# A selective-scan block on one core: two tokens to a partition, and one transfer of 1 KB rows where there were two of 512 B

## The reference

```python
xn = _layernorm(x)
# branch 1: a state-space block with E = 256 channels, N = 64 states, followed by a gated FFN
normed = rmsnorm(xn, input_norm_w)
x_z, z = split(normed @ in_proj_W)                 # (8, 512, 256) each
xc = silu(conv(x_z, conv_W) + conv_b)              # 4 taps
dt = clip(softplus(xc @ dt_W + dt_b), 0.001, 0.1)
Bp, Cp = xc @ B_W, xc @ C_W                        # 64 states each
h_t = exp(dt_t * A) * h_{t-1} + dt_t * B_t * x_t   # 512 steps, state 256 x 64 per sequence
y_t = sum_n h_t * C_t
y = y * silu(z)
x1 = xn + y @ out_proj_W
n2 = rmsnorm(x1, ffn_norm_w)
branch1 = x1 + (silu(n2 @ gate_W) * (n2 @ up_W)) @ down_W
# branch 2: three layers with +-1 weights, 256 -> 512 -> 512 -> 128, relu between
branch2 = binary_mlp(xn)
out = x + branch1 + branch2
```

## Time and profile before

| | |
|---|---|
| median of 3 runs | 1047.95 us (1047.13 to 1048.22) |
| the profiled execution's own time | 1046.38 us |
| its span, first to last instruction | 1044.6 us |
| granted TensorE clock, mean over the span | 0.981 |
| busy, of the span | PE 90%, DVE 87%, ACT 86%, POOL 79% |
| busy share of the DMA engines through the recurrence | 0.95 to 0.98 |

### The profile page before, as it was taken

How to read it: one execution, slowest core, us unless ns; L and a number is a source line. 1 busy time by engine, 2 the same in 40 slices (tenths; PEclk the granted TensorE clock), 3 DMA queues, 4 the chain that set the end, 5 groups by cost and what they waited for, 6 DMA issues and landing times.

```text
span 1044.6 us, 24920 instructions
## 1 busy us (share of the span) xinstructions
PE 941.4 (90%) x8006; PEld 423.2 (41%) x8006; DVE 911.8 (87%) x1966; ACT 902.2 (86%) x1061; POOL 824.3 (79%) x1159
## 2 busy tenths in 40 slices
PE   5999984669999999999999999999999999999997
PEld 3566541123434343434333333434343434343436
DVE  5788965899999999999999999999999999999982
ACT  1766876799999999999999999999999999999981
POOL 5365325899898988898989888888888888989880
PEclk9999996799999999999999999999999999999999
DMA  6265479999999999999999999999999998999940
GB/s 180 79 232 214 166 256 368 365 370 373 372 348 387 341 376 355 372 351 380 346 376 354 371 353 378 351 372 342 384 348 382 344 384 327 389 342 385 351 147 11
DMA packets 86447, 337.39 MB, mean 323 GB/s; under 512 B 15536, under 2 KB 39984, under 8 KB 50992
## 3 DMA queue, kind: packets, MB, share of 16 engines
q1 hardware_dynamic: 86288, 335.70, 86.7%
q10 hardware_dynamic: 32, 0.10, 0.0%
HBM read 308.48 MB, written 27.26 MB: 321 GB/s over the span
## 4 chain that ended last, share of the span: by engine, by line
PE 58%; DVE 16%; POOL 11%; issue 8%; ACT 3%; DMA 2%; SPq 1%; DVEq 0%; POOLq 0%; ACTq 0%
PE ps L817 17%; PE ps L902 11%; PE ps L762 9%; POOL decayed L621 9%; DVE state L1272 8%; DVE ps L1263 5%; PE ps L916 5%; PE ps L669 5%; PE ps L698 3%; PE ps L888 2%; PE ps L880 2%; PE ps L710 1%; POOL f_nrm L633 1%; DMA decay<-dt_stage 1%; DVE h L1354 1%
## 5 line engine op out<-in xcount | busy, mean ns | idle before, releaser
L621 POOL TENSOR_TENSOR decayed<-decay,state 128x256 f32<-128x256 f32 x1024 | 732.4, 735 | 107.9 <-DVE state L1272 82.9
L1035 ACT ACTIVATE decay<-decay,a_col 128x2048 f32<-128x2048 f32 x256 | 515.4, 2013 | 8.9 <-DMA decay<-dt_stage 8.9
L1272 DVE TENSOR_TENSOR state<-decayed,ps 128x256 f32<-128x256 f32 x1024 | 417.7, 417 | 40.4 <-POOL decayed L621 25.5
L1263 DVE TENSOR_TENSOR ps<-decay,ps 128x512 f32<-128x512 f32 x512 | 354.1, 692 | 26.9 <-PE ps L762 9.0
L817 PE MATMUL ps<-state,c_cols 128*32 128x256 f32 x4096 | 331.5, 396 | 2.2 <-issue 0.2
L1047 ACT COPY state<-ps 128x512 f32<-128x512 f32 x512 | 291.2, 594 | 48.5 <-issue 42.2
L762 PE MATMUL ps<-moving,b_rows 64*128 64x256 bf16 x1024 | 200.0, 276 | 64.8 <-DVE ps L1263 61.2
L769 PE MATMUL ps<-moving,b_rows 64*128 64x256 bf16 x1024 | 202.4, 279 | 10.3 <-DMA b_rows<-b_stage 10.3
L902 PE MATMUL ps<-h,w 128*128 128x256 f32 x512 | 172.4, 422 | 0.8 <-DVE h L1354 0.8
L762 PEld LDWEIGHTS ps<-moving,b_rows 64*128 64x128 bf16 x1024 | 59.9, 94 | 230.7 <-issue 138.4
L817 PEld LDWEIGHTS ps<-state,c_cols 128*32 128x32 f32 x4096 | 81.7, 108 | 113.2 <-issue 104.1
(11 more groups left out here) (118 smaller groups left out, 761.8 us busy)
## 6 DMA issues: line engine op xcount, KB each, us to landing
decay<-dt_stage SPq DMA_DIRECT2D x512, 512.0 KB, 6.2
moving<-u_stage SPq DMA_DIRECT2D x64, 256.0 KB
u_stage<-u_parts SPq DMA_DIRECT2D x16, 512.0 KB, 3.1
b_rows<-b_stage SPq DMA_DIRECT2D x64, 128.0 KB
b_stage<-b_parts SPq DMA_DIRECT2D x16, 384.0 KB, 3.0
dt_stage<-dt_tok SPq DMA_DIRECT2D x8, 512.0 KB, 3.9
moving<-u_stage SPq DMA_DIRECT2D x126, 32.0 KB
x_tok<-in_L_attn_x_dram SPq DMA_DIRECT2D x4, 512.0 KB, 4.5
```

The lines of the kernel that those rows point to most:

```text
L621: nc.gpsimd.tensor_tensor(decayed[:, p], decay[:, dec_slot(m, k), p, k % TS, :], state[:, (k - 1) % RING, p * E:(p + 1) * E], ALU.mult).th ...
L1035: nc.scalar.activation(pair, pair, ACT.Exp, scale=a_col[:, 2:3]).then_inc(decay_ready, 1)
L1263: nc.vector.tensor_tensor(ps[:, acc_bank(m, k), :].rearrange("p (q e) -> p q e", q=HQ), decay[:, dec_slot(m, k), HQ:Q, k % TS, :], ps[:, a ...
L1272: nc.vector.tensor_tensor(state[:, k % RING, p * E:(p + 1) * E], decayed[:, p], ps[:, SELFP + k % 2, p * E:(p + 1) * E], ALU.add).then_inc ...
```

## The change

Tokens that follow one another now share a partition. Partition (b, r) of a group holds tokens 2r and 2r+1 of sequence b, tile i being the one with tokens 2r+i. In DRAM these two rows lie side by side, so one DMA with rows of 256 floats, 1 KB, moves what two moved before. That holds for x, for xn and for the result.

The recurrence still hands over y by 16 steps. So the transposes of `y_tok` now write their 128 columns to where these tokens belong: for a token with even number in the first tile's columns, for one with odd number 128 columns further on. Two columns that come out of TensorE one after the other lie 512 bytes apart. `silu_z` is laid out in the same new order, and the ScalarE instruction that writes it does so with the same distance between neighbours. The product that reads both finds them as before, in runs. The number of elements of each of these instructions stays as it was, and so does all the arithmetic.

```diff
-        silu_z = sb("silu_z", [P, EH, NC, B, TC])
+        silu_z = sb("silu_z", [P, EH, NG, GT, B, TG // GT])
...
+        y_feat = ps[:, FA, :].rearrange("e (h i b j r) -> e h i b j r", h=EH, i=GT, b=B, j=GT)
...
-                    for j in range(GT):
-                        sp.dma_start(x_in[:, j, :], x[:, bass.ds(g * TG + j * TC, TC), :]
-                                     ).then_inc(G["f_x_loaded"], 16)
-                    for j in range(GT):
-                        sp.dma_start(xn[:, j, :], xn_stage[:, bass.ds(g * TG + j * TC, TC), :]
-                                     ).then_inc(G["f_xn_loaded"], 16)
+                    for dst, src, loaded in ((x_in, x, "f_x_loaded"), (xn, xn_stage, "f_xn_loaded")):
+                        sp.dma_start(dst[:].rearrange("p j d -> p (j d)"),
+                                     src[:, bass.ds(g * TG, TG), :].rearrange("b (r j) d -> b r (j d)", j=GT)
+                                     ).then_inc(G[loaded], 16)
...
-                    for j in range(GT):
-                        sp.dma_start(out[:, bass.ds(g * TG + j * TC, TC), :], result[:, j, :]
-                                     ).then_inc(G["f_stored"], 16)
+                    sp.dma_start(out[:, bass.ds(g * TG, TG), :].rearrange("b (r j) d -> b r (j d)", j=GT),
+                                 result[:].rearrange("p j d -> p (j d)")).then_inc(G["f_stored"], 16)
...
-                                m = nc.tensor.transpose(ps[:, FA, (h * GT + j) * P:(h * GT + j + 1) * P],
+                                m = nc.tensor.transpose(y_feat[:, h, :, :, j].rearrange("e i b r -> e b r i"),
                                                         y_tok[:, j, h * P:(h + 1) * P], ident[:])
...
-                    nc.scalar.activation(silu_z[:, :, :, n, :], ps[:, ZB[n % 3]:ZB[n % 3] + EH, :]
-                                         .rearrange("p h (c t) -> p h c t", t=TC), ACT.Silu
+                    nc.scalar.activation(silu_z[:, :, :, :, n, :].rearrange("p h g i r -> p (h g) r i"),
+                                         ps[:, ZB[n % 3]:ZB[n % 3] + EH, :].rearrange("p h t -> p (h t)")
+                                         .rearrange("p (g r i) -> p g r i", g=EH * NG, i=GT), ACT.Silu
                                          ).then_inc(S["z_ready"], 1)
...
-                            silu_z[:, :, bass.ds(g * GT, GT)].rearrange("e h c b t -> e h (c b t)"), ALU.mult
+                            silu_z[:, :, g].rearrange("e h j b r -> e h (j b r)"), ALU.mult
```

More of the change, by code:

```diff
@@ L538, in _ @@
                 store(NG - 1)
-                sp.wait_ge(G["f_stored"], 16 * GT * NG)
+                sp.wait_ge(G["f_stored"], 16 * NG)
             @block.gpsimd
@@ L635, in finish @@
                     if k == K_BASE:
-                        pool.wait_ge(G["f_x_loaded"], (g + 1) * (16 * GT))
+                        pool.wait_ge(G["f_x_loaded"], (g + 1) * 16)
                         after(pool, "f_x1_ready", g)
@@ L831, in finish @@
                     if k == K_XN_T:
-                        pe.wait_ge(G["f_xn_loaded"], (g + 1) * (16 * GT))
+                        pe.wait_ge(G["f_xn_loaded"], (g + 1) * 16)
                         after(pe, "f_hid_ready", g, back=1)
@@ L1361, in finish @@
                         after(dve, "f_base", g)
-                        after(dve, "f_stored", g, per=16 * GT, back=1)
+                        after(dve, "f_stored", g, per=16, back=1)
                         nc.vector.tensor_tensor(result[:].rearrange("p j d -> p (j d)"), ps[:, FB, 0:GT * D],
```

## The result

The change makes the kernel slower by 0.18%: the ratio to before is 1.0018, with a 95% interval of 1.0012 to 1.0024, which is 1.9 us (1.3 to 2.5). The medians are 1049.51 us over 22 runs and 1047.97 us over 22 runs of before. One execution differs from the next by more than this, so a pair of profiles has to be read with care. The profiled execution of after took 1051.27 us by its own time, that of before 1046.38.

What follows compares the result with a forecast made beforehand. The prediction took the recurrence, a loop over four engines, to bound the kernel, not DMA. Its terms summed 0 - 0.4 + 0 + 0 = -0.4 us, giving a forecast of 1047.5 us, range 1045.6 to 1050.8.

Steps and rivals of the forecast that it cites:

- What bounds the kernel: Whole kernel: the recurrence over four engines sets the pace; DMA engines at share 0.98 are full but not awaited.
- the third rival: Decay loads in the bodies: the queue was thin, 1.8 us of DMA waits vanish, 1045.8 us; chance 0.12, or more gain included.
- SP's queue, 0: DMA issues in the bodies: 2.25 us a body saved, all hidden by SP's wait for VectorE, so 0.
- The end, -0.4 us: Last store: one issue of 0.62 us goes, 64 KB more to land costs 0.18 us; gain taken as 0.4 us.
- The transposes of y, 0: TensorE's four transposes a group: scattered PSUM writes cost nothing, taken as 0; upper end 2.9 us, 7 us without cover.
- The writes of silu_z, 0: Eight ScalarE instructions, three without slack ahead of the recurrence: scattered writes cost 0; 1.2 us the case next to it.
- the first: Rival on silu_z: scattered ScalarE writes cost time, 1.2 us (chance 0.12) or 3.3 us (chance 0.06).
- its dearer measure: Silu writes judged against L1077: 1.08 ns an element, +3.3 us for three instructions, 1050.8 us; chance 0.06.
- its cheaper one: Silu writes judged against L1071: 0.38 ns an element, +1.2 us for three instructions, 1048.7 us; chance 0.12.
- the signs of being wrong: Four transposes over 0.9 us, recurrence's first step over 1 us later, or a body shorter by 0.15 us or more.
- the DMA case: Decay loads in the bodies, same as the third rival: -1.8 - 0.4, 1045.8 us; named as the range's low end, 1045.6.

Runs made afterwards that it cites:

- dma_only: The kernel before with the merged transfers alone, transposes and silu in the old order: ratio 1.0000 to before (0.9991 to 1.0008), 1047.34 us.
- first3: The changed kernel where only the first three silu instructions write at 512 bytes, the other five writing runs: ratio 1.0017 to before (1.0008 to 1.0025).
- last5: The changed kernel where only the last five silu instructions write at 512 bytes, the first three writing runs: ratio 1.0000 to before (0.9992 to 1.0009).
- the probes: Two versions of the changed kernel, each of eight silu instructions writing or reading in its own pattern: 1.02 us in one run, 2.01 at 16 bytes.
- swap_again: The changed kernel with the silu instruction's two inner loops swapped so it writes runs, second measurement: ratio 0.9994 to before (0.9985 to 1.0003), 1047.49 us.
- after_again: The changed kernel as it is, measured again on the same chip as swap_again: ratio 1.0015 to before (1.0006 to 1.0024), 1049.54 us.

## Why the prediction was wrong, point by point

**What bounds the kernel: right.** The DMA share of 0.98 did not mean a wait. With half the token transfers, the bodies kept their 816.5 us; dma_only, where they take 816.6 us (204.2 to 1020.8), shows the same by itself. The 1.8 us of waits for decays that the third rival wanted to win are no test of it, since they come and go.

**SP's queue, 0: right.** 29.8 us of issues, where 16 x 2.25 = 36 had been counted, went into longer waits for VectorE, as the waiting in the earlier trace rows had suggested.

**The end, -0.4 us: right in kind, too large.** One issue went, 0.58 us (1.24 to 0.66). The wait behind it grew from 1.6 to 2.0 us, and 0.2 us are left: 3.34 us from the last result to the end before, 3.17 after, 3.12 in dma_only. The term that was too small is the landing of the added 64 KB, 0.18 us as I had it, 0.4 us measured. The way of counting of the Trainium skill, "DMA: Bandwidth & Descriptors", section "Why a DMA increments its semaphore by 16 and not by 1", had given an estimate of 0.36 us for it and a gain of 0.26 us. That is nearer; how many DMA engines took part was not shown by any run.

**The transposes of y, 0: right.** Four of them take 0.66 us where they took 0.65. Writing PSUM from TensorE at 512 bytes between neighbours costs these fp32 transposes nothing. The rule of the Trainium skill, "PSUM — Partial Sum Buffer", section "Specifications (TRN2)", that spoke against it doesn't hold for this case, and ScalarE's reads of PSUM at a distance are free as well. My reason, that a column of an fp32 transpose takes two cycles anyway (0.86 ns at 2.4 GHz), fits, but was not tested: no run here had TensorE write such a pattern at a column a cycle. The same kind of reason failed for ScalarE, so it is no more than a guess.

**The writes of silu_z, 0: this is the step that failed.** The text had the place right: three instructions without slack, the five behind them covered, as first3 and last5 show (+2.06 us and +0.04 us). The range was right too, 0 to 1.1 us for each. The value that I took from it, 0, was wrong. Measured are 0.98 us for each, nearly the end that L1077 gave (1.08 ns an element, measured 0.96). I set aside the only row with a scattered write, L1018, for its other differences, and argued that 1 ns an element leaves room for a second line. It does not: 0.96 ns came on top for each. What the probes show in its place: an element alone in its 16 bytes costs ScalarE about 1.9 to 2.0 ns instead of 1.0. In L1018 too each write stood alone (132 bytes), and its excess over L1077, 138 ns for 128 elements, is 1.08 ns for each; L1071, which I put beside it first, scales by a column and is longer for that reason or another, not known here.

The path took 2.2 us to the cast, 2.1 us to SP's first load of decays and 2.4 us to the first exponential, not 3 x 0.98 = 2.9. Before, the two casts had started 0.08 and 0.10 us after ScalarE was through with silu, when VectorE had their inputs ready, at 146.16 by this row of before and at 148.62:

```profile
144.93 1.23 DVE L1182 TENSOR_TENSOR u_tok<-ps,dt_tok 128x1024 f32<-128x1024 f32 x1
```

Now ScalarE sets the time, and back to back its records overlap by some 0.2 us (150.28 + 1.98 is 152.26, the cast starts at 152.04). From the first silu to the first cast it takes 3.57 us instead of 2.02, and from there to the second 3.06 instead of 2.41. So 0.4 us of the two times 0.98 are taken up in the first stretch, and 0.3 us of 0.98 in the second.

**The sum.** 0 - 0.2 + 0 + 2.2 = 2.0 us, where the ratio gives 1.9 (1.3 to 2.5), and swap_again against after_again 2.05 for silu alone. No part of the result beyond this interval is left over. Of the rivals, the first was the right one, with its dearer measure. I had given it 0.06 and its cheaper one 0.12. Its time of 1050.8 us was 1.3 us too high, for the most part because the path took 2.2 of its 3.3 us. My range reached that far only because of these rivals; by the mechanism that I forecast the time would have fallen by 0.4 us. Of the signs of being wrong that I had named, one came: the recurrence starts over 1 us later. One small slip changes nothing: the low end of the range, 1045.6, was called the DMA case, whose sum is 1045.8.

## What to carry to other kernels

A layout change that makes transfers longer gives a step to whoever writes or reads the new order. Give it to the side that takes it for nothing. Here these were reads, of PSUM by ScalarE or of SBUF by VectorE with two neighbours to 16 bytes, and not single fp32 writes to SBUF. In one instruction this is only a matter of which loop is inside. When a cost is unknown and the only row near it is imperfect, it still beats an argument. Ask first whether the instruction has slack: of eight equally slow ones, three cost 2 us here and five cost nothing. Fewer DMA issues were worth no time in the bodies here, since nobody waited for the queue that issues them.

## What was not expected of the hardware

- ScalarE's writes to SBUF cost by the neighbours that share 16 bytes: 1.02 us for 1024 fp32 in a run, 1.12 at 8 bytes, 1.58 at 12, 2.01 at 16, and not more than 2.12 in any row at a greater distance. Runs of two at 16 bytes are nearly free, 1.11.
- Steps on the reading side cost nothing in any row here: ScalarE from PSUM at 8 bytes to 2 KB, 1.01 to 1.02 us; VectorE from SBUF at 8 bytes, 0.68 us.
- TensorE's fp32 transposes write PSUM at 512 bytes between neighbours at their old pace, 0.65 to 0.66 us for four in the bodies.
- A last store of 128 KB in 1 KB rows was awaited for 2.0 us behind its issue, two of 64 KB in 512-byte rows for 1.6 us behind the second's.
